# A four-layer graph network: scatter-adds moved from the first stage into the second and issued one at a time, without crosswise merging, and a second ScalarE one-hot in every other step

## The reference

```python
# layer 0: sum of the 32 edge attributes by source node, then a two-layer perceptron with batch norm
agg = segment_sum(edge_attr_32, src, 3125);  x = x + mlp(concat(h, agg))
# layer 1: a message for every edge from the row of its source node, summed by destination
R = relu(edge_weight[:, None] @ w1 + b1) @ w2 + b2
Fj = h[src];  msg = tensor_product(R, spherical_harmonics(edge_attr_3), Fj)
x = x + zeros.at[dst].add(msg)
# layer 2: three rounds with the weighted adjacency, normalized by weighted degree, and a clip
for _ in range(3): out = clip(segment_sum(norm[:, None] * out[src], dst, 3125) * 0.9 + 0.1 * h, 0, 1)
# layer 3: three rounds with the adjacency of counts and self-loops, relu, batch norm
for i in range(3): z = batchnorm(relu(segment_sum(wn[:, None] * z[src], dst, 3125)))
```

## Time and profile before

| what | value |
|---|---|
| median of 3 runs | 3463.08 us (3460.28 to 3467.24) |
| the profiled execution | 3467.37 us, span 3465.3 us |
| busy: PE, VectorE, ScalarE, GpSimd | 86%, 79%, 66%, 62% |
| indirect adds (L585) | 782, 1333.0 us busy, mean 1705 ns |
| indirect gathers (L593) | 782, 760.8 us busy, mean 973 ns |
| DMA | 388.67 MB, mean 112 GB/s |

### The profile page before, as it was taken

How to read it: one execution, slowest core, us unless ns; L and a number is a source line. 1 busy time by engine, 2 the same in 40 slices (tenths; PEclk the granted TensorE clock), 3 DMA queues, 4 the chain that set the end, 5 groups by cost and what they waited for, 6 DMA issues and landing times. The chain is left out here.

```text
span 3465.3 us, 69301 instructions
## 1 busy us (share of the span) xinstructions
PE 2974.6 (86%) x19703; PEld 2370.4 (68%) x19703; DVE 2742.9 (79%) x6018; ACT 2280.7 (66%) x3192; POOL 2141.3 (62%) x1629
## 2 busy tenths in 40 slices
PE   3888788988856999999999999999999976657657
PEld 3677677777745888888888888888888851113257
DVE  6678988888856999999999999999999973441065
ACT  3678688888836888888888888888888842220000
POOL 4048888888877777777777777777777730000000
PEclk9899899999977999999999999999999997798778
DMA  9943222222222333333333333333333359998940
GB/s 400 419 154 38 12 15 15 15 16 16 15 25 41 53 53 52 50 53 51 50 53 51 50 53 51 51 53 52 50 53 52 50 187 426 426 391 342 373 172 6
DMA packets 265695, 388.67 MB, mean 112 GB/s; under 512 B 149903, under 2 KB 200838, under 8 KB 259254
## 3 DMA queue, kind: packets, MB, share of 16 engines
q0 software_dynamic: 149184, 120.78, 20.7%
q1 hardware_dynamic: 100034, 195.42, 16.6%
q10 hardware_dynamic: 16416, 71.74, 5.1%
HBM read 260.01 MB, written 127.78 MB: 112 GB/s over the span
## 5 line engine op out<-in xcount | busy, mean ns | idle before, releaser
L585 POOL DMA_INDIRECT both<-kept x782 | 1333.0, 1705 | 439.8 <-issue 194.6
L923 PEld LDWEIGHTS ps<-prod,big 128*128 128x128 f32 x7840 | 1133.9, 190 | 137.7 <-DVE prod L1290 133.0
L923 PE MATMUL ps<-prod,big 128*128 128x170 f32 x7840 | 1183.2, 310 | 22.5 <-DVE prod L1290 17.4
L593 POOL DMA_INDIRECT kept<-feat_dram,kept x782 | 760.8, 973 | 243.2 <-issue 233.1
L668 ACT ACTIVATE big<-iota_b,kept 128x640 f32<-128x640 f32 x1029 | 779.0, 815 | 13.6
L914 PE MATMUL ps<-prod,onehot 128*128 128x320 f32 x3920 | 684.5, 325 | 81.2 <-DVE prod L1320 79.6
L914 PEld LDWEIGHTS ps<-prod,onehot 128*128 128x128 f32 x3920 | 597.7, 194 | 112.9 <-DVE prod L1320 84.5
L673 ACT ACTIVATE big<-big 128x2560 f32<-128x2560 f32 x196 | 458.0, 2337 | 277.2 <-PE ps L923 277.1
L988 PE MATMUL ps<-w2mix,kept 65*128 65x384 f32 x1568 | 559.3, 500 | 21.7 <-ACT kept L720 20.4
L1462 DVE TENSOR_REDUCE kept<-kept 128x80 f32<-128x1280 f32 x392 | 561.4, 1471 | 0.0
L988 PEld LDWEIGHTS ps<-w2mix,kept 65*128 65x128 f32 x1568 | 284.2, 191 | 179.7 <-issue 25.5
(11 more groups left out here) (235 smaller groups left out, 3028.9 us busy)
## 6 DMA issues: line engine op xcount, KB each, us to landing
both<-big POOLq DMA_DIRECT2D x40, 1910.0 KB, 91.2
big<-both SPq DMA_DIRECT2D x24, 1600.0 KB, 11.8
big<-both SPq DMA_DIRECT2D x24, 1528.0 KB, 13.2
kept<-keys_dram SPq DMA_DIRECT2D x196, 128.0 KB, 3.0
kept<-in_wT SPq DMA_DIRECT2D x196, 128.0 KB
adj_c<-kept ACTq DMA_DIRECT2D x42, 400.0 KB, 31.6
kept<-adj_c SPq DMA_DIRECT2D x9, 1600.0 KB, 22.4
adj_w<-kept ACTq DMA_DIRECT2D x16, 800.0 KB, 33.6
```

The source lines that it names most:

```text
L585: pool.indirect_dma_start(both, bass.IndirectOffsetOnAxis(ap=sc_idx[:, c:c + 1], axis=0), sc_val[:, c // 2, c % 2, :], None, compute_op=AL ...
L593: pool.indirect_dma_start(gath[:, s % 2, k, :], None, feat_dram, bass.IndirectOffsetOnAxis(ap=src_i[:, 4 * s + k:4 * s + k + 1], axis=0)). ...
L923: mm = pe.matmul(part_sums(part, MSG), onehot[:, q, k, part * P:(part + 1) * P], prod[:, q, k, 0:HI * MSG], start=False, stop=False, skip_ ...
```

## The change

- `by_act`: ScalarE makes two of the four one-hots in steps with k4 = 0 and 2 (before: only with k4 = 3), VectorE the rest.
- GpSimd issues 372 adds ahead of the first gather in place of 392 (`AHEAD`). In the second stage an add stands before the second and before the fourth gather of every step, from the first step on; in every 16th step (`MIX`) one stands before each gather, as far as an add's data are two steps old. So the 20 are caught up.
- The second stage compares a chunk only with itself: half of ScalarE's comparison columns, two of six small matmuls per step gone. Two neighbouring chunks may now hit one place, so from chunk 392 on every add waits until the one before it has landed.
- Some waits that another wait implies are left out: in the first stage three of four adds no longer wait for their data, in the second stage every other one.

```diff
+AHEAD, MIX = 372, 16
...
-            return (0, 1) if k4 == 3 else (0,)
+            return (0, 1) if k4 % 2 == 0 else (0,)
...
             def add(c):
-                pool.wait_ge(s_idx, c // 2 + 1)
+                if c < CH // 2 and c % 4 == 0:
+                    pool.wait_ge(s_idx, c // 2 + 2)
                 if c >= CH // 2 and c % 2 == 0:
-                    pool.wait_ge(s_add[1], 16 * (c // 2))
-                if c >= 2:
+                    pool.wait_ge(s_idx, c // 2 + 1)
+                if c >= CH // 2:
+                    pool.wait_ge(s_add[(c - 1) % 2], 16 * ((c + 1) // 2))
+                if 2 <= c <= CH // 2:
                     pool.wait_ge(s_add[c % 2], 16 * (c // 2))
...
-            for c in range(CH // 2):
+            for c in range(AHEAD):
                 add(c)
+            added = AHEAD
+            def add_next(s):
+                if added < min(USED, 2 * (STEPS + s - BEHIND) + 2):
+                    add(added)
+                    return added + 1
+                return added
             pool.wait_ge(s_feat, 16)
-            gather(0, range(4))
+            for k in range(4):
+                gather(0, k)
             for s in range(STEPS + BEHIND):
-                if s + 1 < STEPS:
-                    gather(s + 1, range(min(4, USED - 4 * (s + 1))))
-                if s >= BEHIND:
-                    for c in range(2 * (STEPS + s - BEHIND), min(2 * (STEPS + s - BEHIND) + 2, USED)):
-                        add(c)
+                for k in range(4):
+                    if k % 2 or s % MIX == MIX - 1:
+                        added = add_next(s)
+                    if s + 1 < STEPS and 4 * (s + 1) + k < USED:
+                        gather(s + 1, k)
+            for c in range(added, USED):
+                add(c)
...
-                    act.activation(key_gap[:, 2 * i * P:(2 * i + 2) * P], keyrow[:, q, 0:2 * P], ACT.Square, scale=-1.0,
+                    act.activation(key_gap[:, i * P:(i + 1) * P], keyrow[:, q, i * P:(i + 1) * P], ACT.Square, scale=-1.0,
...
-                    for i in range(2):
-                        lo = 0 if (i, j) == (0, 1) else 1
-                        mm = pe.matmul(o[:, j, lo:7], same[:, q, 2 * i + j, :],
-                                       wparts[:, ds(2 * d + i, 1), lo:7].rearrange("p c v -> p (c v)"),
-                                       start=False, stop=(i == 1), skip_group_check=True)
+                    mm = pe.matmul(o[:, j, 1:7], same[:, q, j, :],
+                                   wparts[:, ds(2 * d + j, 1), 1:7].rearrange("p c v -> p (c v)"),
+                                   start=False, stop=True, skip_group_check=True)
```

More of the change, by code:

```diff
@@ L586, in add, with gather @@
                                         sc_val[:, c // 2, c % 2, :], None, compute_op=ALU.add).then_inc(s_add[c % 2], 16)
-            def gather(s, ks):
-                if s >= 2:
+            def gather(s, k):
+                if s >= 2 and k == 0:
                     pool.wait_ge(s_terms, 2 * (s - 1))
[L592 to L595, removed]
+                pool.indirect_dma_start(gath[:, s % 2, k, :], None, feat_dram,
+                                        bass.IndirectOffsetOnAxis(ap=src_i[:, 4 * s + k:4 * s + k + 1], axis=0)
+                                        ).then_inc(s_gath[s % 2], 16)
             pool.wait_ge(s_zeroed, 16 * (ZERO_PIECES + 1))
             pool.wait_ge(s_zeroed, 16 * (ZERO_PIECES + 1))
-            for c in range(CH // 2):
+            for c in range(AHEAD):
                 add(c)
+            added = AHEAD
[4 more added lines that the diff above has]
+                return added
             pool.wait_ge(s_feat, 16)
-            gather(0, range(4))
+            for k in range(4):
+                gather(0, k)
             for s in range(STEPS + BEHIND):
-                if s + 1 < STEPS:
-                    gather(s + 1, range(min(4, USED - 4 * (s + 1))))
-                if s >= BEHIND:
-                    for c in range(2 * (STEPS + s - BEHIND), min(2 * (STEPS + s - BEHIND) + 2, USED)):
-                        add(c)
+                for k in range(4):
[5 more added lines that the diff above has]
+                add(c)
             eighths = both[0:TABLE, :].rearrange("(s d) o -> s (d o)", d=EIGHTH)
@@ L659, in compare @@
                 act.wait_ge(s_ded, d - 1)
-                act.activation(same[:, q, 0:4, :].rearrange("p b e -> p (b e)"), key_gap[:, 0:4 * P], ACT.Relu,
+                act.activation(same[:, q, 0:2, :].rearrange("p b e -> p (b e)"), key_gap[:, 0:2 * P], ACT.Relu,
                                scale=-1.0, bias=1.0).then_inc(s_same, 1)
@@ L857, in merge @@
                 for j in range(2):
-                    pe.matmul(o[:, j, 0:1], same_tri[:, q, j, :], ones_bf[:, :], start=(j == 0), stop=False,
+                    pe.matmul(o[:, j, 0:1], same_tri[:, q, j, :], ones_bf[:, :], start=(j == 0), stop=True,
                               skip_group_check=True)
-                    for i in range(2):
-                        lo = 0 if (i, j) == (0, 1) else 1
-                        mm = pe.matmul(o[:, j, lo:7], same[:, q, 2 * i + j, :],
-                                       wparts[:, ds(2 * d + i, 1), lo:7].rearrange("p c v -> p (c v)"),
-                                       start=False, stop=(i == 1), skip_group_check=True)
+                    mm = pe.matmul(o[:, j, 1:7], same[:, q, j, :],
+                                   wparts[:, ds(2 * d + j, 1), 1:7].rearrange("p c v -> p (c v)"),
+                                   start=False, stop=True, skip_group_check=True)
                 mm.then_inc(s_ded, 1)
@@ L1267, in mark_earlier @@
                 dve.wait_ge(s_ded, d - 1)
-                V.tensor_tensor(same_tri[:, q, 0:2, :], same[:, q, 0:4:3, :], earlier[:, :].unsqueeze(1).broadcast_to([P, 2, P]),
+                V.tensor_tensor(same_tri[:, q, 0:2, :], same[:, q, 0:2, :], earlier[:, :].unsqueeze(1).broadcast_to([P, 2, P]),
                                 ALU.mult).then_inc(s_tri, 1)
```

## The result

The changed kernel takes 3495.6 us (median of 5 runs, 3486.72 to 3503.95) against 3463.08 for the kernel before: a ratio of 1.0091 with a 95% interval of [1.0067, 1.0115], slower by some 32 us. Measured again beside the later experiments (e9) the ratio was 1.0117 [1.0095, 1.0140]. The forecast was 3493.

What follows compares the result with a forecast made beforehand. GpSimd's list was taken as the chain that bounds from 212 us to the second stage's end. Terms -43.9 + 40.6 + 21 + 17 - 4.9 = +30 us gave 3497 against the profiled execution, 3493 against the median; range 3465 to 3514.

Steps and rivals of the forecast that it cites:

- Twenty adds leave the head of the list: Before the first gather: 20 fewer adds let GpSimd gather from 1013.6 in place of 1057.58, -43.9 us.
- Twenty-one more adds stand between: Between first and last gather: 405 adds against 384, each costing issue and gap, 1.93 us; +40.6 us.
- Changing kind costs: Second-stage steps: alternating single adds with pairs of gathers lengthens instructions, 0.11 us over 195 steps; +21 us, ends 0 and 33.
- An add waits for the landing: 16th steps: adds behind one gather stall 0.64 us at 40 places; two thirds taken, +17 us, ends 8 and 26.
- GpSimd's early waits: Start of the second stage: adds now fill four gathers' waits for VectorE's reads, -4.9 us.
- At nothing: Second stage: halving ScalarE's comparison and dropping two small matmuls per step gains nothing, as GpSimd holds the steps at 8.95.
- the first gather near 1012: Start of the second stage: sign that the forecast is right; near 1030 would mean the first stage gave nothing.
- gathers of 1.01 and 0.98: Second stage: sign that the forecast is right, gathers taking these us in turn, with adds of 1.61 to 1.65.
- steps of 9.05: Second stage: sign that the forecast is right, steps of 9.05 us or more; steps near 8.7 would refute it.
- The rival in which changing kind costs nothing: Second stage: steps could run at 8.67 us, 55 us less over 195 steps, total 3415; chance 0.12.
- a gain of up to 9 us from fewer one-hots on VectorE: First stage: less locking of the shared port would speed the 372 adds, total 3484; left in the bound.
- its fixed 2.0 us: Second-stage landing waits: this fixed DMA cost from issue start would remove the landing term, total 3476; rejected on the trace.

Runs made afterwards that it cites:

- e1: The kernel before with only the first-stage one-hots split anew (ScalarE two of four at k4 = 0 and 2): 3467.57 us, 0.9975.
- e5: The kernel before with only the two adds of each second-stage step set apart, before the second and fourth gather: 3471.98 us, 0.9987.
- e11: The changed kernel with 388 adds ahead and no 16th steps, so every second-stage add stands behind two gathers, second measurement: 3451.86 us, 0.9955.
- e3: The changed kernel with 388 adds ahead and no 16th steps, so every second-stage add stands behind two gathers, first measurement: 3453.85 us, 0.9937.
- e8: The kernel before with only the first half's waits for merged data thinned, every fourth add waiting for its group: 3455.14 us, 0.9961.
- e2: The changed kernel with the one-hot split of the kernel before: 3529.81 us, 1.0156.
- e10: The changed kernel catching up in every 8th step in place of every 16th, second measurement: 3513.7 us, 1.0134.
- e4: The changed kernel catching up in every 8th step in place of every 16th, first measurement: 3516.09 us, 1.0116.

## Why the prediction came out right

The total was right (3493 against 3495.6, inside the range, slower as forecast), and the reason that carries it held: GpSimd's list is the chain, and moving adds along it returns what it takes. That the total came within 3 us is luck: one term was 21 us too high and another 14 too low. The second measurement, 1.0117, would be 3504 us, 11 above the forecast and still inside the range.

- *"Twenty adds leave the head of the list"*, -43.9: measured -48.3. The table had to come 16 us sooner and came 33 sooner, with 20 estimated; e1 shows the one-hots do that. The start went to 1009.28, and not the table but the adds held it. The 4.4 us more are the waits left out, less somewhat slower adds.
- *"Twenty-one more adds stand between"*, +40.6: held, 40.5 with 4.6 more for a longer mean.
- **The step that failed: *"Changing kind costs"*, +21.** The rows of before showed longer first gathers behind a *pair* of adds, and the prediction gave that price to every single add. (The 1.61 and 1.58 of its adds came from one step: over the stage of before the first and the second add of a pair take 1.626 and 1.625.) A gather behind a single add takes 0.98, the next 0.95, and e5 puts the whole term at nothing or a little below (0.9987, upper end 1.0002). The lower bound that was kept, 0, was the value.
- *"An add waits for the landing"*, +17: mis-sized, 31.0 measured. The 40 places were right and each paid 0.69 over the gap in place of the 0.64 reckoned (39.8 us less 40 gaps, 27.6 us); the third that was taken off, on the ground that an add with a wait fewer may follow the landing more closely, had no support and was not there. The rest, 3.3, are waits ahead of eight adds behind two gathers. e11 beside e9 shows that waits and longer adds come with the catching up, and go with it.
- *"GpSimd's early waits"*, -4.9: held, no gather of the changed kernel waits for VectorE's reads.
- *"At nothing"*, ScalarE and TensorE: held as far as the runs go: e3 and e11, which have both, lose nothing by it. The waits left out, put into a bound, were worth more than thought: e8 gives 0.0039 of the time alone, some 13 us (9 between the medians), at the start.
- Not foreseen: the tail, 5.5 us, of which 1.7 come and go from run to run. The other engines' steps were left out of the sum because GpSimd is full; at the end of the stage it is VectorE's and TensorE's last step, not GpSimd's, that the third stage waits for.
- The range: its own lower edge, 3465, is not the sum of the ends that it names. With a start at -52, nothing for the order and 8 for landings they give -52 + 40.6 + 0 + 8 - 4.9 = -8, that is 3455.

Of the signs named ahead, the first gather near 1012 and the full GpSimd came; gathers of 1.01 and 0.98 did not, nor steps of 9.05: an ordinary step takes 8.90 and only the 16th is long. Nor did VectorE wait for gathers in nearly every step: it did in 88 of 196, after 120 before. The rival in which changing kind costs nothing had its premise right and its price wrong: adds and gathers did not fall to 1.54 and 0.94.

The SBUF — State Buffer page of the Trainium skill (Who interferes with whom) was weighed for a gain of up to 9 us from fewer one-hots on VectorE. The first stage of the changed kernel (lines, 212 to 940 us) shows none: with 415 one-hots in 728 us where 456 stood in 766, the adds' mean is 1809 ns after 1795. Nor do the other traces: over all adds ahead of the first gather the mean is 1.780 to 1.815 us in the nine with the new one-hots and 1.777 to 1.878 in the four with the old.

```profile
L589 POOL DMA_INDIRECT both<-kept x341 | 616.8, 1809 | 283.2 <-DMA both<-big 172.2 <-issue 106.1 <-DMA both<-kept 4.9
L1324 DVE TENSOR_SCALAR onehot<-iota_b,kept 128x640 fp32r<-128x640 f32 x415 | 221.2, 582 | 0.0
```

The other page of the Trainium skill that was weighed, DMA: Bandwidth & Descriptors (Anatomy of one DMA — SWDGE path), would have made the landing waits vanish by its fixed 2.0 us; the trace had 3.89 us from one add's start to the next that waits for it, and has 3.85 now (1447.57 to 1451.42). The measurement decides.

## What to carry to other kernels

An engine at 79% busy can be full: add the fixed gap before each of its instructions before calling it idle, and then moving work from one place of its list to another gains nothing by itself, even where it lets the next stage start 48 us sooner. A wait for a landing is free where enough other work stands between the two (two gathers, 2.85 us with the gaps, here) and costs 0.6 to 0.75 us each time behind one; so give every such add two gathers (e11) rather than catch up in bursts. And leave out waits that an earlier wait implies: alone that gave 0.9961 [0.9945, 0.9977], most of what the best version here has over the kernel before (e11, 0.9955; e3, 0.9937).

## What the runs showed of the hardware

**TensorE's clock fell behind each 16th step.** Windows of the changed kernel around the 16th step shown above (length, PE, PEld, DVE, ACT, POOL busy, then the granted clock), and the timelines of VectorE and PE:

```profile
1464.00:1470.00 6.00, 3.83 (x26) 3.22 (x25) 2.58 (x9) 4.01 (x5) 4.78 (x5) 1.00 0.29 37
1470.00:1476.00 6.00, 4.57 (x8) 1.91 (x8) 5.76 (x12) 1.32 (x3) 4.66 (x5) 0.59 0.37 69
1476.00:1482.00 6.00, 5.79 (x23) 5.79 (x24) 5.88 (x15) 3.12 (x5) 4.90 (x4) 0.55 0.17 25
1482.00:1490.00 8.00, 8.00 (x51) 6.90 (x50) 6.08 (x17) 5.12 (x8) 6.17 (x7) 1.00 0.27 32
```

```profile
1467.42 0.26 DVE L1446 TENSOR_TENSOR kept<-kept 128x96 f32<-128x96 f32 x1 [6.34 <-DMA kept<-feat_dram,kept]
```

```profile
1461.14 6.03 PE L936 MATMUL ps<-prod,big 128*128 128x170 f32 x40 [0.24 <-DVE prod L1303]
...
1476.21 8.54 PE L936 MATMUL ps<-prod,big 128*128 128x170 f32 x40 [1.49 <-DVE prod L1303]
```

VectorE waits 6.34 us for the delayed gather, TensorE is busy 3.83 of 6 us, and then the granted clock is 0.59 and 0.55 in the next two windows of 6 us, so most of that time it is at the lower of its two levels, 1.2 and not 2.4 GHz; 40 matmuls take 8.54 us in place of 6.03. After that it is back. It is not this one step alone: of the 196 message sums of the changed kernel 14 took 7.4 to 9.0 us, one behind each of the twelve 16th steps (granted clock 0.56 to 0.80 over 7 us), the first of the stage and the last. In e11, without 16th steps, it is the first and the last alone, and the granted clock is 1.00 from 1200 to 2780 us. In the middle of the stage this costs nothing that the trace shows: no gather of the changed kernel waits for VectorE, so GpSimd's list goes on at its own pace. In the tail it does count: the stretch of the last sums has 0.79, and they took the 7.68 us seen above. Neither the stalled step nor the change is the cause there: e11, which has no 16th step, and e1, which has the second stage of before, took 7.68 us for them too, and e3, the same kernel as e11, took 6.01, as the kernel before did behind 2.30 us of idle TensorE. What decides it from run to run stays open.

```profile
2842.00:2850.00 8.00, 7.68 (x40) 7.45 (x40) 0.13 (x2) 0.00 (x0) 0.53 (x1) 0.79 0.06 0
```

**Open.** The adds' mean in the first stage was 1889 ns in e2 and 1809 in the changed kernel, and 1789 in e8, which has e2's one-hots; so the one-hots do not explain it, and no run here tells what does. And the third stage was six us shorter in e10 than in e9, as in e4, with its code unchanged, from the first load to the end of the span (2862.51 to 3502.6 against 2852.18 to 3498.4). The changed kernel's first trace had 643.5, so part of this is the difference of one run from another; no run says why the rest.
